# One wait per unit for the gathers of a DLRM tower kernel

## The reference

```python
e = jnp.stack([tbl_0[ids[:, 0]], ..., tbl_31[ids[:, 31]]], axis=1)
for W in (W0, W1):
    prev = x.shape[1]
    z = jnp.einsum('bhd,bmd->bhmd', inputs, x).reshape(b, n * prev, k)
    x = jnp.einsum('bpd,pj->bjd', z, W)
    res.append(x)
out = jnp.sum(jnp.concatenate(res, axis=1), axis=-1)
...
h = jnp.concatenate([z, dense_ctx], axis=1)
h = jnp.maximum(h @ W_top1 + b_top1, 0.0)
h = jnp.maximum(h @ W_top2 + b_top2, 0.0)
y = h @ W_top3
```

## Time and profile before

| | us |
|---|---|
| median of 3 runs | 499.83 |
| lowest, highest | 497.79, 503.77 |
| the profiled execution, its own time | 505.6 |
| span of the profiled execution | 503.8 |

### The profile page before, as it was taken

The page is one execution under the profiler, slowest core; times in us unless marked ns, Lnnn a source line. Parts: engine busy times, 40 slices in busy tenths (PEclk is TensorE's granted clock), DMA queues, the critical chain, the costliest instruction groups (busy, mean ns, idle before and its releaser), DMA issues.

```text
span 503.8 us, 9536 instructions
## 1 busy us (share of the span) xinstructions
PE 393.6 (78%) x3656; PEld 348.6 (69%) x3656; DVE 203.3 (40%) x834; ACT 235.1 (47%) x774; POOL 251.6 (50%) x262
## 2 busy tenths in 40 slices
PE   4679742279788887788887887788778788799998
PEld 3457641168677766786786876676668677699988
DVE  4026971733243434334444432343324444445310
ACT  2258641076343634464444543373446444466621
POOL 5734877554565555556654555565546665400000
PEclk9779965568898979999888978897998988899999
DMA  8300000000000000000000000000000000000000
GB/s 277 128 4 12 8 14 13 5 10 10 11 13 10 12 12 10 9 12 12 12 10 9 12 10 10 10 12 11 10 12 11 10 12 10 11 3 2 1 2 1
DMA packets 10765, 9.66 MB, mean 19 GB/s; under 512 B 4664, under 2 KB 8896, under 8 KB 10720
## 3 DMA queue, kind: packets, MB, share of 16 engines
q0 software_dynamic: 8192, 4.21, 5.6%
q1 hardware_dynamic: 2528, 4.84, 2.8%
HBM read 9.03 MB, written 0.00 MB: 18 GB/s over the span
## 4 chain that ended last, share of the span: by engine, by line
PE 58%; ACT 16%; issue 12%; DVE 8%; another core or an unknown queue 4%; DMA 1%; SPq 0%; ACTq 0%
PE WA L745 20%; ACT TS L305 8%; PE PA L707 7%; PE QB L717 7%; PE T L730 6%; DVE RT L441 5%; PE M L758 4%; ACT eblk L305 4%; PE M L777 3%; PE PA L659 2%; PE QB L664 2%; PE ET L694 2%; ACT h L378 2%; ACT eT L305 1%
## 5 line engine op out<-in xcount | busy, mean ns | idle before, releaser
L298 POOL DMA_INDIRECT emb<-in_table,rows x256 | 251.0, 980 | 189.5 <-PE T L730 58.7
L745 PE MATMUL WA<-TS,RX 128*128 128x128 f32 x896 | 127.5, 300 | 2.8 <-issue 1.7
L604 DVE COPY TS<-T 32x64 f32<-32x64 f32 x256 | 55.3, 216 | 175.8 <-PE T L730 158.6
L745 PEld LDWEIGHTS WA<-TS,RX 128*128 128x128 f32 x896 | 119.5, 213 | 8.2 <-issue 8.1
L717 PE MATMUL QB<-eblk,zQ 128*64 128x68 f32 x1024 | 55.9, 234 | 48.7 <-issue 48.6
L717 PEld LDWEIGHTS QB<-eblk,zQ 128*64 128x64 f32 x1024 | 42.5, 141 | 60.8 <-issue 57.1
L305 ACT ACTIVATE eblk<-ET 32x256 f32<-32x256 f32 x128 | 48.7, 381 | 75.7 <-PE ET L694 66.3
L707 PE MATMUL PA<-eblk,zP 128*128 128x132 f32 x512 | 79.6, 293 | 3.3 <-issue 1.4
L572 DVE TENSOR_TENSOR zQ<-ET,eT 128x1024 f32<-128x1024 f32 x32 | 39.2, 1225 | 89.6 <-ACT eT L305 80.0
L707 PEld LDWEIGHTS PA<-eblk,zP 128*128 128x128 f32 x512 | 72.1, 209 | 4.3 <-issue 2.8
L305 ACT ACTIVATE TS<-PA 128x396 f32<-128x396 f32 (+1 forms) x96 | 44.5, 463 | 60.0 <-remote 51.9
(11 more groups left out here) (87 smaller groups left out, 290.5 us busy)
## 6 DMA issues: line engine op xcount, KB each, us to landing
emb<-in_table,rows POOLq DMA_INDIRECT x256
TS<-in_W SPq DMA_DIRECT2D x8, 256.0 KB, 3.9
wt<-in_W_top SPq DMA_DIRECT2D x2, 512.0 KB
y1w<-in_W_rows SPq DMA_DIRECT2D x1, 448.0 KB
TS<-in_W_rows SPq DMA_DIRECT2D x1, 448.0 KB
sym<-in_W_cols SPq DMA_DIRECT2D x1, 264.0 KB
TS<-in_W_cols SPq DMA_DIRECT2D x1, 264.0 KB
idc<-in_ids SPq DMA_DIRECT2D x1, 128.0 KB, 2.1
```

The source lines that it names most:

```text
L298: eng.indirect_dma_start(emb[par][:, g, :], None, table, bass.IndirectOffsetOnAxis(rows[:, k, g:g + 1], 0))\
L604: eng.tensor_copy(view(ts[32 * q:32 * q + 32, :, :], P * REST + b0, [[4 * P, 2], [P, 4], [1, 8]]), view(src, q, [[C17, 2], [4, 4], [C33, 8 ...
L745: m = eng.matmul(WA[:, 0:P], C[:, kt, :], TS[k % 2][:, slot_of(kt), :], start=(kt == 0), stop=(kt == KT - 1))
```

## The change

`pace(n)` is changed and nothing else. With x the number of the gather in pace unit u:

- gathers x = 0 to 7 wait for `t3_made >= u`, the end of unit u - 1; for u = 0 there is no wait. From pace unit 4 on these are all the gathers of the unit.
- the two further gathers of pace units 0 to 3 (x = 8 and 9) wait for `p_made >= 3u + 2`.

```diff
                 u, x = divmod(n, 10) if n < 10 * UNITS else divmod(n - 2 * UNITS, UG)
-                if x < 3:
-                    eng.wait_ge(p_made, TRIOS * u + 1)
-                elif x < 6:
+                if n < 10 * UNITS and x >= UG:
                     eng.wait_ge(p_made, TRIOS * u + 2)
                 else:
-                    eng.wait_ge(t3_made, u + 1)
+                    wait(eng, t3_made, u)
```

## The result

The changed kernel takes 542.13 us (median of 4 runs, 539.3 to 543.17) against 499.78 for the kernel before (here the median of 4 runs): ratio 1.082, 95% interval 1.075 to 1.089. The profiled executions took 542.64 and 505.6. The forecast was 567, with 540 to 600 as its own range.

What follows compares the result with a forecast made beforehand. PE was taken as the bound, with gathers costing it 19.2 us per tile. +59 for units 4 to 26 and +8 for the setup made +67 on 499.83, giving 567 us, range 540 to 600 (8 in 10: 518 to 620).

Steps and rivals of the forecast that it cites:

- the hold: From about an unbroken row's third gather, PE's counts go unreported and PE soon stops, until 11.9 us into the unit.
- The rule of no contention: Skill's rule that DMAs never contend with compute engines: gathers would cost PE nothing, sum 0, time 500; the forecast overrode it.
- First unit: First unit of each tile: second bank's count held; 11.9 + 1.8 + 0.7 = 14.4 us, against 11.25 before.
- an ACT copy inside the row: Sign that the forecast is wrong: ACT copies the second bank while POOL is still in its row of gathers.
- Second and third unit: Second and third units of each tile: ET's count passes, first bank's comes near the hold's end; 16.0 us, against 15.15 and 14.19.
- Fourth unit: Fourth unit of each tile: `hidden1` held too, its followers run one after another; 18.5 us, at least 17.7, against 14.00.
- Setup: Before the steady units: a longer POOL run, then eight gathers over PE's constant transposes; +8 us, from +4 to +13.
- The lower end of my sum: Smallest total for a tile's four units: 14.4 x 3 + 17.7 = 60.9 us, 6.3 more than before.
- The deeper hold: Rival: ET's count is held in three units of four; 600 to 634 us, chance 0.17.
- no change: Rival: each gather takes 0.6 us from PE wherever it stands, so moving them changes nothing; 500 us, chance 0.05.
- The weaker one: Rival: all at the lower ends, 540 us, or 525 if part of second and third units stays at 14.2; chance 0.10.
- The faster one: Rival: the hold stops PE but not ACT; units about 13 us, 493 us in all, chance 0.08.

Runs made afterwards that it cites:

- e1: The changed kernel with the gathers of tiles 2 to 7 left out, so POOL is idle from unit 4 on: 398.68 us.
- e2: The changed kernel with all eight gathers of a unit put behind its first bank step, still in one row: 573.48 us.
- e3: The changed kernel with the old gates (three, three and two gathers) back in the fourth unit of each tile alone: 535.09 us.
- e11: The changed kernel, gates kept, each gather also waiting until the one two places before has landed, across unit ends too: 476.73 us, ratio to the kernel before 0.955.
- e6: The changed kernel with the gathers of tiles 2 to 7 replaced by plain DMAs of 128 rows issued by POOL: 398.03 us.
- e7: The changed kernel with the gathers of tiles 2 to 7 replaced by plain DMAs of 128 rows issued by SP: 397.82 us.
- e4: The kernel before with gathers in pairs behind the three bank steps and T3 (three, three, four in pace units 0 to 3): 493.06 us, ratio 0.981.
- e12: As e11, but without the gates on PE's progress from unit 4 on: 544.3 us, ratio to the kernel before 1.079.
- e9: The changed kernel with a short POOL fill, waited for, behind every second gather: 542.66 us.

## Why the prediction was right, and where it was off

**The cause stood.** The forecast was slower because unbroken rows hold PE's counts, and e1, e2, e3 and e11 show it from both sides: without gathers or with spaced ones the wait is gone, with later or longer rows it grows. The second bank's copy and L715 in unit 12 are as forecast, with the hold ending 254.09 - 242.46 = 11.6 us after the unit's start, where 11.9 was taken.

**The rule of no contention.** By rows, a tile took 54.59 us with gathers and 35.40 without, and e1 has now put 36.33 beside it in the same place. The Trainium skill, "SBUF — State Buffer", section "Who interferes with whom", says that a DMA never contends with a compute engine. For the plain DMAs of e6 and e7 the trace agrees (36.3 us a tile). For indirect ones the gathers' cost is there all the same. But the section speaks of SBUF ports, and no run here shows that a port is what PE waits for: what the traces show is late counts and a PE that stands. I had stretched the rule to all that a DMA can do to PE.

**First unit.** 14.4 forecast, 13.86 measured. ACT's count of the second bank came at 251.27, while the row's last gather had yet to start, and not at the hold's end. So T3's matmuls came 1.1 us after the hold's end, with no wait for ACT, where I had added 1.8; they themselves took 1.1 us, not 0.7, for the granted clock was 0.50 of full from 254.09 to 256.30, behind 5.4 us in which PE had mostly stood. The prediction had named an ACT copy inside the row as a sign against it; it was one against the sharp end of the hold, not against the hold.

**Second and third unit.** This is the step that failed: 16.0 forecast, 14.08 and 14.05 measured. I held that ET's count would get through but the first bank's come near the end of the hold. Neither was held. ET's matmuls came 2.2 us after the unit's start (258.53), since L743's fourteen took 2.45 us and not 2.9 or more, and the first bank's copy went straight behind ACT's copies out of ET. The hold does not set in at a fixed gather: a count 3.5 us into the row was held in unit 12, and one that fell 4.5 us into another row, at 138.5, passed. The floor of 14.4 that I had worked out was itself the answer. This is 3.9 us of a tile.

**Fourth unit.** 18.5 forecast, 19.23 measured. ACT's h began 11.67 us into the unit (11.9 taken), and from there to T3's end it was 7.56 us and not 5.8. The granted clock was 0.50, the lower of its two levels (1.2 and 2.4 GHz), from 296.12 to 301.90, behind 3.8 us in which PE had stood; in the rows that gave the 5.8 it had been 1.00 (275.71 to 281.30 of the kernel before), and `hidden2` took 3.78 us in place of 2.05. That L715 would creep here too ("the fourth included") was wrong, and it contradicted my own chain, in which L715 comes behind `hidden2`.

**Setup.** +8 forecast, +0.7 measured. POOL's long run ended 3.4 us later and the next gathers began 3.9 us later, as worked out:

```profile
93.03 0.94 POOL L296 DMA_INDIRECT emb<-in_table,rows  x1 [0.30 <-issue]
99.47 4.03 POOL L296 DMA_INDIRECT emb<-in_table,rows  x1 [5.49 <-PE T L728]
```

But unit 2 took 34.1 us (29.1 before) and unit 3, over which the eight gathers lie, 19.9 (23.0 before): the row cost PE's transposes no more than the four gathers and the pauses had, rather less.

**The sum.** Forecast +59 for the tiles and +8 for the setup; measured +36.4 and +0.7. Of the 30 us too much, 21 are the units' 3.7 us a tile times 5.75 (0.5 + 1.9 + 1.95 - 0.7), 7 the setup, and the rest is what the other tiles differ from this one. The lower end of my sum, 60.9 us a tile, came within half a microsecond of the 61.2 measured. The bound was right and the value chosen inside it wasn't. Some of this is luck: in that end the first three units were 0.3 to 0.5 us too long and the fourth 1.5 too short. And that 542.13 lies inside 540 to 600 hangs on how the two kernels are compared. By the medians the loss is 42.35 us, by the profiled executions 37.0, which is below the +40 that was the lower bound on just these; the one profiled before was 5.8 us slower than its median.

**The rivals.** The deeper hold (600 to 634) and no change fell. The weaker one was nearest: 540 against 542.13. The faster one needed the second bank's count at 4 us into the row; it came at 8.5.

## What to carry to other kernels

Here indirect DMAs from POOL that follow one another closely delayed the semaphores of TensorE's matmuls and stopped TensorE between them, though nobody waited for the rows; so when PE shows "issue" idle and ACT "remote" waits, look for a row of gathers beside them. Gates on another engine's progress moved such a row or broke it, but kept no distance between gathers (493.06 us at best, e4). What helped was to tie each gather to the landing of the one two places before and to keep the gates as well (e11, 476.73 us); the tie without the gates was 544.3 (e12). Count the instructions rather than the bytes, and see in the trace that the pace you wanted is the one you got.

## What the runs showed of the hardware

- The hold belongs to indirect DMAs and not to their bytes: 64 rows each gave 548.07 us, 128 rows 542.13, and the same number of plain DMAs 398.03 from POOL and 397.82 from SP. The plain ones made shorter rows (4.21 and 4.68 us against 9.7).
- The hold goes with the pace. At 1.25 and at 1.33 us between gathers (the changed kernel, e9) the times are 542.13 and 542.66; at about 1.6, in pairs 1.3 apart with 1.8 between them (e11), it is 476.73 and L720 never creeps. That the pace alone does it is not shown.
- A gather's instruction on POOL is 0.94 us long, and its packets end 2.05 us after its start (median), in a held stretch as well as elsewhere. So the transfers aren't what is late in a hold. The Trainium skill, "Perfetto Trace Analysis", section "DMA Instruction — SWDGE (GPSIMD)", says that the end shown for such an instruction is that of making descriptors and not of moving the data; the trace agrees.
- What in the chip passes PE's counts late, and what makes PE stand at L715, stays open. No run here reaches below the semaphores.
